# Exponentials written into the score bank, and one broadcast product that scales both row blocks

## The reference

```
x = x + 0.5 * ffn(layernorm(x))      # dense 512x512 + top-2 of 8 LoRA experts
x = x + attention(layernorm(x))
x = x + 0.5 * ffn(layernorm(x))
```

```
q, k, v = rope(x @ wq), rope(x @ wk), x @ wv
scores  = q k^T / sqrt(128), masked to (j <= i) & (j > i - 128)
out     = softmax(scores) v
return out @ wo
```

## Time and profile before

| | |
|---|---|
| runs (median; lowest to highest) | 746.7 us (746.32 to 746.92), 3 runs |
| profiled execution, first to last instruction (its span) | 744.6 us |
| TensorE matmul, busy | 717.2 us, 96% |
| VectorE, busy | 601.0 us, 81% |
| ScalarE, busy | 413.3 us, 56% |
| GpSimd, busy | 396.5 us, 53% |
| granted TensorE clock, mean | 0.998 of full speed |
| chain that ended last | TensorE 70%, VectorE 20%, issue 5%, ScalarE 3% |

### The profile page before, as it was taken

One profiled execution on the slowest core, in us unless ns is written; L12 is line 12 of the kernel. 1 busy time (PEld: TensorE's weight loads), 2 busy tenths in 40 slices (PEclk: granted clock), 3 DMA queues, 4 the chain that ended last, 5 costly groups with the idle time before them and its releaser, 6 DMA issues.

```text
span 744.6 us, 13949 instructions
## 1 busy us (share of the span) xinstructions
PE 717.2 (96%) x3692; PEld 603.1 (81%) x3692; DVE 601.0 (81%) x2060; ACT 413.3 (56%) x1122; POOL 396.5 (53%) x466
## 2 busy tenths in 40 slices
PE   8899789999999999999999999999999999998998
PEld 5787667888888888888888888888888888887786
DVE  6898778877887888878887888788878887788795
ACT  3324475657655676556655766576656665754320
POOL 0674268634864477438653765367535863462420
PEclk9999999999999999999999999999999999999999
DMA  8240003100220022002200120013000310030002
GB/s 266 73 158 16 0 3 98 43 1 2 73 70 1 0 70 70 0 0 70 56 14 0 56 70 14 0 32 94 15 0 0 99 28 1 1 114 1 0 31 85
DMA packets 25843, 32.13 MB, mean 43 GB/s; under 512 B 5833, under 2 KB 14281, under 8 KB 25298
## 3 DMA queue, kind: packets, MB, share of 16 engines
q1 hardware_dynamic: 25232, 30.69, 13.1%
q10 hardware_dynamic: 578, 1.05, 0.4%
HBM read 27.54 MB, written 4.19 MB: 43 GB/s over the span
## 4 chain that ended last, share of the span: by engine, by line
PE 70%; DVE 20%; issue 5%; ACT 3%; DMA 1%; POOL 1%; DVEq 0%; SPq 0%; ACTq 0%
PE bank L1102 26%; PE bank L1160 19%; PE bank L1145 6%; PE bank L1124 5%; PE bank L1068 5%; PE bank L1132 3%; DVE prob L822 2%; DVE rot L787 2%; DVE oT_lo L834 2%; DVE prob L814 1%; DVE sm L807 1%; PE bank L1121 1%; DVE rot L778 1%; ACT prob L550 1%; DVE pT_hi_lo L828 1%
## 5 line engine op out<-in xcount | busy, mean ns | idle before, releaser
L368 POOL TENSOR_TENSOR swap<-swap,rope 128x512 f32<-128x512 f32 x80 | 110.1, 1377 | 129.8 <-ACT swap L523 129.8
L550 ACT ACTIVATE prob<-sm,nmax 128x128 f32<-128x128 f32 x128 | 51.5, 403 | 151.4 <-DVE prob L814 150.4
L375 POOL TENSOR_SCALAR_AFFINE_SELECT pT_hi_lo<-pT_hi_lo 128x256 fp32r<-128x256 f32 x128 | 52.3, 409 | 140.3 <-DVE pT_hi_lo L828 139.8
L523 ACT ACTIVATE swap<-bank 64x512 f32<-64x512 f32 x160 | 94.9, 593 | 10.6 <-PE bank L1102 6.7
L558 ACT ACTIVATE pT_hi_lo<-bank 128x256 fp32r<-128x256 f32 x128 | 48.9, 382 | 71.5 <-PE bank L1132 50.6
L822 DVE TENSOR_SCALAR prob<-prob,rinv 128x128 f32<-128x128 f32 x256 | 83.3, 367 | 4.5
L385 POOL TENSOR_TENSOR q_lo<-rot,q_hi 128x512 fp32r<-128x512 f32 x64 | 82.6, 1291 | 6.9 <-ACT q_hi L531 6.9
L1160 PE MATMUL bank<-wo_hi,oT_hi 128*128 128x512 f32 x256 | 74.6, 413 | 5.0 <-DVE x L841 5.0
L828 DVE TENSOR_TENSOR pT_hi_lo<-bank,pT_hi_lo 128x256 fp32r<-128x256 f32 x128 | 53.6, 418 | 29.4 <-ACT pT_hi_lo L558 29.2
L1102 PE MATMUL bank<-xnT_hi,wq_hi 128*128 128x512 f32 x256 | 71.4, 391 | 2.2 <-DVE v_lo L798 1.4
L1102 PE MATMUL bank<-xnT_lo,wq_hi 128*128 128x512 f32 x256 | 73.4, 389 | 0.0
(11 more groups left out here) (150 smaller groups left out, 1768.9 us busy)
## 6 DMA issues: line engine op xcount, KB each, us to landing
raw<-in_L_attn_wq SPq DMA_DIRECT2D x32, 256.0 KB, 3.0
raw<-in_L_attn_wo SPq DMA_DIRECT2D x32, 256.0 KB, 2.6
x<-in_L_attn_x SPq DMA_DIRECT2D x4, 512.0 KB, 7.3
raw<-in_L_attn_wk SPq DMA_DIRECT2D x8, 256.0 KB, 2.7
raw<-in_L_attn_wv SPq DMA_DIRECT2D x8, 256.0 KB, 2.6
out<-x SPq DMA_DIRECT2D x8, 256.0 KB, 2.0
raw<-in_L_ffn_W_base ACTq DMA_DIRECT2D x4, 256.0 KB, 5.1
wb_keep_hi<-q_hi SPq DMA_DIRECT2D x1, 1024.0 KB, 4.9
```

What stands on the lines that cost most here:

```text
L368: nc.gpsimd.tensor_tensor(w, w, tab, ALU.mult).then_inc(t2_done, 1)
L523: last = nc.scalar.activation(swap[a:a + half, m % 2, :], A[m % 2][b:b + half, :], ACT.Copy)
L550: last = nc.scalar.activation(prob[:, s % 2, lo:hi], src, ACT.Exp, bias=nmax[:, s % 2, i:i + 1], scale=-1.0, accum_out=rsum[:, s % 2, i:i ...
```

## The change

Before, ScalarE writes the two exponentials of a unit into the SBUF tile prob, and two products on VectorE scale them in place, each with one column of rinv as the scalar. After, ScalarE writes them into the first 256 columns of the unit's own score bank S[s % 2], which VectorE has read by then, and one product on VectorE reads both blocks from there, with rinv broadcast along the columns, and writes prob. Three waits move with it. ScalarE no longer waits for the transpose of unit u - 2 (t_done), since it does not write prob any more; VectorE's product waits for it instead. And TensorE may write bank S anew only when the product has read it, so `scores` waits for norm_done of unit u - 1, where it waited for min_done of that unit; the same goes for the router of the second feed-forward block, which also writes S.

```diff
             def softmax_exp(u, s):
                 act.wait_ge(min_done, u + 1)
-                wait(act, t_done, u - 1)
                 for i, (lo, hi) in enumerate(((0, P), (P, 2 * P))):
                     src = prob[:, s % 2, 2 * P:3 * P] if i else sm[:, s % 2, 0:P]
-                    last = nc.scalar.activation(prob[:, s % 2, lo:hi], src, ACT.Exp,
+                    last = nc.scalar.activation(S[s % 2][:, lo:hi], src, ACT.Exp,
                                                 bias=nmax[:, s % 2, i:i + 1], scale=-1.0,
                                                 accum_out=rsum[:, s % 2, i:i + 1])
                 last.then_inc(exp_done, 1)
...
                 dve.wait_ge(rinv_done, u + 1)
-                for i, (lo, hi) in enumerate(((0, P), (P, 2 * P))):
-                    last = nc.vector.tensor_scalar(prob[:, s % 2, lo:hi], prob[:, s % 2, lo:hi],
-                                                   rinv[:, s % 2, i:i + 1], None, ALU.mult)
-                last.then_inc(norm_done, 1)
+                wait(dve, t_done, u - 1)
+                nc.vector.tensor_tensor(prob[:, s % 2, 0:2 * P].rearrange("p (c n) -> p c n", c=2),
+                                        S[s % 2][:, 0:2 * P].rearrange("p (c n) -> p c n", c=2),
+                                        rinv[:, s % 2, :].unsqueeze(2).broadcast_to([P, 2, P]),
+                                        ALU.mult).then_inc(norm_done, 1)
...
                     if f == 1 and pr == 0:
-                        pe.wait_ge(min_done, 16 * KV - 1 + i)
+                        pe.wait_ge(norm_done, 16 * KV - 1 + i)
...
                 pe.wait_ge(qlo_done, 5 * j + 2 + h)
-                wait(pe, min_done, u - 1)
+                wait(pe, norm_done, u - 1)
```

## The result

The changed kernel takes 739.6 us (739.08 to 740.12, 4 runs), the kernel before 746.81 us (746.32 to 747.28, 4 runs): a ratio of 0.9898, 95% interval 0.9884 to 0.9912, 7.2 us less. The forecast was 740.9 us, 5.8 us less. The profiled execution spans 738.4 us, of which 1.07 us are a later start: the first transposes of V (L1111), ahead of which almost nothing was changed, begin at 87.54 us, and at 86.47 us in the trace of before. So stretches are compared, not ends.

A forecast was written before the change was run, and what follows sets the result against it. TensorE, busy 96% of the span, was taken as the bound. Gains of 4.1 (looped groups), 1.4 (first group) and 0.3 (attention's end), 5.8 us, took the span from 744.6 to 738.8, median 740.9 us; range 739.2 to 746.5.

The forecast's parts named there:

- The mechanism: Looped groups: an unheld product lets unit 6's rotary sum run before GpSimd's wk_lo; x_add ends at 196.6 instead of 198.06 us.
- the prediction's last part: List of signs of right or wrong; one for right was GpSimd's wk_lo starting about 0.4 us later.
- the term 6 x 0.69 = 4.1 us: Six looped groups: TensorE's 0.69 us wait for x_add goes in each, 4.1 us gained.
- The exponentials, counted as nothing: ScalarE's exponentials written to a bank: at most 0.05 us either way for each, counted as no gain or loss.
- The rule of the Trainium skill weighed in the prediction: VectorE's product: fp32 input in PSUM is slower, making the new product 0.14 us slower than the old pair.
- The first group: First group: TensorE waits less for L778 (0.95 of 1.07 us) and for x_add (0.21 instead of 0.68), together 1.42 us.
- The last group: End of the attention, chain through VectorE and ScalarE: some five products at 0.06 us each, 0.3 us gained.
- The new wait of scores: TensorE's scores of unit u + 1 wait for the product of unit u - 1; cost: nothing.
- the covers: First group and last half: TensorE's existing waits for p_lo before transposes, 0.83 and 1.26 us, absorb the scores' new wait.
- The stall: Rival, chance 0.12: unit 6's rotary sum loses against wk_lo in every group, x_add stays late; 746.4 us.
- The smaller gain: Rival, chance 0.17: product 0.50 us, exponentials 0.05 us more each, rotary sum misses its gap in some groups; 743.3 us.
- The slower rival: Rival, chance 0.07: exponentials into a bank 0.15 us longer or more, rotary sum misses its gap before wk_lo; 750.3 us.

The follow-up runs named there:

- wk_lo's shift: The kernel before, old products kept, with GpSimd making wk_lo after unit 6 instead of unit 5: 740.01 us, ratio 0.9915.
- the one product from SBUF: The kernel before with one broadcast product in place of two, exponentials left in SBUF and waits unchanged: 740.44 us, ratio 0.9917.
- shown alone: The kernel before with only the wait of scores changed from min_done to norm_done, also at the second feed-forward router: 746.52 us, ratio 1.0002.
- the copies: The changed kernel with one, three or five useless ScalarE copies between each unit's two exponentials: 740.04, 741.91 and 756.19 us.

## Why the prediction was right in its mechanism and short in its size

**The mechanism** held in each step. The product with an input in the bank is not held; it takes 0.42 us, the value taken. Set against the output projection's first part (191.70 in the trace of before, 268.14 after, a shift of 76.44 us), the rotary sum starts at 193.28 (forecast 193.2) and ends at 194.06 (193.88), and x_add ends at 196.81 (196.6). It got in ahead of wk_lo, while `p_part` (L375) ran. wk_lo did not start later, as the prediction's last part had it; it starts 1.62 us after GpSimd's product against 1.64 before, and its record is 0.44 us longer instead.

**The step that failed is the term 6 x 0.69 = 4.1 us.** It measured 5.5 us. The price of the wait was read as the idle time between two busy intervals, and the start of the second is an event while the end of the first is modelled. The trace of before has both cases, the transpose and then the output projection's first weight load and matmul behind it, without a wait and with it:

```profile
191.56 0.38 PE L1132 MATMUL bank<-ident,prob 128*128 128x128 f32 x2
191.67 0.76 PEld L1160 LDWEIGHTS bank<-wo_hi,oT_hi 128*128 128x128 f32 x4
191.70 1.17 PE L1160 MATMUL bank<-wo_hi,oT_hi 128*128 128x512 f32 x4
...
197.14 0.38 PE L1132 MATMUL bank<-ident,prob 128*128 128x128 f32 x2
198.18 0.76 PEld L1160 LDWEIGHTS bank<-wo_hi,oT_hi 128*128 128x128 f32 x4 [0.89 <-issue]
```

Without a wait the projection starts 0.14 us after the transpose, well inside its 0.38 us; with it, at 198.21, 1.07 us after. The wait costs 0.93 us, and 6 x 0.93 = 5.6. The changed kernel's pair at 273.58 and 273.72 is at 0.14 again. wk_lo's shift, which touches neither exponentials nor products, gives 5.35 us and so shows that it is the wait's own price. That TensorE was "busy 76.91 us" of a group was the same error, and the forecast of 76.9 us for the group came from it; it is 76.65.

**The exponentials, counted as nothing**, bring nothing. Their records became 0.03 us shorter each, but the reciprocal behind them still starts 0.91 us after the first. So the 1.2 us by which the changed kernel beats the one product from SBUF over the three stretches are not theirs; in the first and the last group they come from the held product, as shown there, and of the 0.39 us in the six looped groups I have not followed the parts. Here the Trainium skill ("ScalarE: Activation LUTs", section "Step-by-step: what each stage is for") says that ScalarE reaches PSUM faster than SBUF; the trace agrees for the record of the instruction, 372 against 403 ns, but not for what waits behind it.

**The product.** The rule of the Trainium skill weighed in the prediction ("VectorE: DVE Perf Modes", section "Why PSUM operands drop a tier" and the section on the TRN2 errata) put the new product at 392 ns and the old pair at 254. The product takes 425 ns, near it. The pair took 0.48 us in SBUF, so the rule's sum of 0.14 us against the change is not borne out; but its other half is: a tensor_scalar loses speed by an input in PSUM, 286 to 348 ns.

**The first group**, forecast 1.42, measured 1.28 us. Set against the start (1.07 us later), `rope_cos` of unit 5 (L777) begins at 110.81 (forecast 110.86) and the rotary sum at 115.55 (115.54). But the sum takes 0.88 us and not 0.74:

```profile
116.62 0.88 DVE L786 TENSOR_TENSOR rot<-rot,swap 128x512 f32<-128x512 f32 x1 [0.78 <-POOL swap L368]
```

That is the missing 0.14 us. TensorE meets new waits on the way, 0.31 and 0.30 us of the scores for the product at 103.12 and 107.52, and 0.48 us of a weight load for wo_lo at 115.39. They cost nothing in the end, since it then still waits for x_add, whose chain runs through VectorE: a weight load idles for 0.26 us ahead of 120.36, where 0.21 had been forecast.

**The last group**, forecast 0.3, measured 0.39 us. From the reciprocal of its eighth unit to the end of the stretch it takes 18.90 us instead of 19.16, which is the 0.06 us for each of some four products that the forecast had in mind; the rest comes earlier. The one product from SBUF has this too (18.92) and loses it before, by the held product shown above. **The new wait of scores**, forecast nothing: nothing, shown alone. The prediction also lists such waits among the signs that it is wrong; they came, 2.5 us in four places, and were no such sign. The forecast of the covers was right as well: the waits of the scores for the product take the place of waits for p_lo behind them, 2.8 for 3.1 us.

**The rivals.** The stall did not move to the rotary sum: GpSimd's `p_part` between its product and wk_lo did not shut VectorE out. The smaller gain failed on both its conditions, 0.50 us for the product and longer exponentials. The slower rival was a wrong picture of the gap, as the copies show: at 0.31 us more per unit, about its 2 x 0.15, the cost is 2.7 us and not the 9.4 us between its 750.3 and the forecast. A large loss does come, but somewhere between 0.31 and 0.51 us per unit, and through other waits.

## What to carry to other kernels

Price a wait of TensorE from the start of the matmul ahead of it to the start of the one that waited, less the same distance where nothing waited; the idle time shown said too little here (0.69 for 0.93 us). Where two engines hold each other up, look at what is queued behind the held instruction and which gap it is aimed at: the same 5 us came from an input moved to a bank, from two instructions made one, and from one number that puts wk_lo a unit later. Such routes don't add up.

## What the runs showed of the hardware that I had not expected

- The record of a ScalarE exponential of 128x128 is shorter into a bank than into SBUF: 403 to 372 ns for the first of a pair, 387 to 352 ns for the second. But the second starts 0.40 us after the first and the reciprocal 0.91 us after it in either kernel.
- Where the input lies sets the time of a tensor_scalar of 128x128 on VectorE (286 ns from SBUF, 348 ns from a bank) but not that of the product of two tensors of 128x256 (426 and 425 ns).
- Both forms are held beside GpSimd's pieces with their input in SBUF (up to 1.33 and 1.12 us), and neither in any instance with it in a bank (354 and 427 ns at most), though the broadcast rinv of the product still comes from SBUF. With its input in SBUF the product holds GpSimd in turn (a product of GpSimd 1.51 instead of 1.29 us).
- A ScalarE copy recorded as 240 ns, set between two exponentials, moves the second by 0.15 us; records of ScalarE overlap, and their sum says too much.
- The step is steep: 0.31 us more for each unit costs 2.7 us by the table, 0.51 us costs 16.2 us.
